# One opening product moved from POOL to DVE, the second group's sums in another order, and the last batch's end chain rewritten

## What is computed

```python
x = x + jnp.tanh(g_xattn[0]) * _L0_xattn_ref(_layernorm(x, axis=-1), ctx_4096, L0_xattn_weight)
x = x + jnp.tanh(g_ffn[0]) * _L0_ffn_ref(_layernorm(x, axis=-1), L0_ffn_router_w, L0_ffn_router_b, L0_ffn_A, L0_ffn_Bm)
```

```python
sim = jnp.stack([_cosine_sim(embedding, emb_l), _cosine_sim(embedding, embedding), _cosine_sim(embedding, emb_r)], axis=1)
...
out = jnp.einsum('bit,oi->bot', inp_unf * att, w_flat)
```

```python
topv, topi = jax.lax.top_k(probs, TOP_K)
...
h = jnp.einsum('nd,erd->ner', flat, A)
hw = h * w[:, :, None]
out = jnp.einsum('ner,eor->no', hw, Bm) * SCALING
```

## Time and profile before

| what | value |
|---|---|
| median of 3 runs | 210.16 us (210.09 to 210.34) |
| the profiled execution's own time | 210.47 us |
| its span in the profile | 208.7 us |
| PE busy, share of the span | 97% |
| DVE, POOL, ACT busy | 79%, 62%, 58% |
| moved by DMA | 26.79 MB, mean 128 GB/s |

### The profile page before, as it was taken

How to read it: one execution, slowest core, us unless ns; L and a number is a source line. 1 busy time by engine, 2 the same in 40 slices (tenths; PEclk the granted TensorE clock), 3 DMA queues, 4 the chain that set the end, 5 groups by cost and what they waited for, 6 DMA issues and landing times.

```text
span 208.7 us, 4522 instructions
## 1 busy us (share of the span) xinstructions
PE 202.4 (97%) x1466; PEld 130.9 (63%) x1466; DVE 165.6 (79%) x426; ACT 121.0 (58%) x233; POOL 129.9 (62%) x222
## 2 busy tenths in 40 slices
PE   8989999999999999999999999999999999999993
PEld 7865657566655647565655646475666666767872
DVE  3375588897979697998979698978879787878663
ACT  4677469668655673755656563845746676632331
POOL 5588654975876756476766438587557576665410
PEclk9999999999999999999999999999999999999999
DMA  6999632150443526151625323220405020202106
GB/s 192 349 375 312 237 117 85 17 190 0 147 158 121 184 102 204 64 191 50 220 81 191 106 112 100 97 108 36 168 0 195 8 104 2 100 0 114 41 0 251
DMA packets 14360, 26.79 MB, mean 128 GB/s; under 512 B 1282, under 2 KB 9602, under 8 KB 14338
## 3 DMA queue, kind: packets, MB, share of 16 engines
q1 hardware_dynamic: 14194, 26.25, 35.5%
q10 hardware_dynamic: 144, 0.26, 0.3%
HBM read 18.12 MB, written 8.39 MB: 127 GB/s over the span
## 4 chain that ended last, share of the span: by engine, by line
PE 87%; POOL 1%; issue 0%; ACT 0%; DVE 0%
PE conv_ps L1087 31%; PE hidden_ps L1138 14%; PE xT_ps L1097 7%; PE sim_ps L1066 5%; PE out_ps L1156 4%; PE hidden_ps L1008 4%; PE out_ps L1157 3%; PE out_ps L1158 3%; PE out_ps L1147 2%; PE conv_ps L1080 2%; PE conv_ps L1083 2%; PE conv_ps L1081 2%; PE xT_ps L1051 1%; PE xT_ps L1021 1%; PE conv_ps L1108 1%; PE out_ps L1183 1%
## 5 line engine op out<-in xcount | busy, mean ns | idle before, releaser
L1087 PE MATMUL conv_ps<-pt,wT 128*128 128x512 f32 x158 | 81.6, 601 | 0.0
L779 DVE TENSOR_TENSOR pt<-xn,sim_ps 128x512 f32<-128x512 f32 x96 | 60.1, 678 | 2.2 <-PE sim_ps L1066 1.6
L574 ACT ACTIVATE xT<-xT_ps 128x512 f32<-128x512 f32 x31 | 18.5, 597 | 38.9 <-PE xT_ps L1097 38.6
L1138 PEld LDWEIGHTS hidden_ps<-aT,xT 128*128 128x128 f32 x248 | 31.9, 190 | 5.5 <-issue 5.1
L1138 PE MATMUL hidden_ps<-aT,xT 128*128 128x136 f32 x248 | 33.7, 279 | 0.0
L428 POOL TENSOR_TENSOR rinv<-nmax,minus_half 128x8 f32<-128x8 f32 x16 | 26.8, 1677 | 6.4 <-DVE nmax L716 6.4
L1087 PEld LDWEIGHTS conv_ps<-pt,wT 128*128 128x128 f32 x158 | 26.1, 196 | 5.1 <-issue 3.1
L419 POOL TENSOR_TENSOR qp<-qp 128x1024 f32<-128x1024 f32 x8 | 19.0, 2381 | 14.9 <-DVE qp L701 14.9
L567 ACT ACTIVATE xn<-xt,offset,rs 128x1024 f32<-128x1024 f32 x16 | 19.8, 1237 | 7.9 <-POOL offset L439 7.6
L1097 PEld LDWEIGHTS xT_ps<-wide,x 128*128 128x128 f32 x124 | 15.3, 140 | 10.3 <-issue 7.9
L786 DVE TENSOR_TENSOR x<-conv_ps,xt 128x512 f32<-128x512 f32 x31 | 21.2, 683 | 0.6 <-PE conv_ps L1087 0.3
(11 more groups left out here) (168 smaller groups left out, 329.6 us busy)
## 6 DMA issues: line engine op xcount, KB each, us to landing
xt<-x SPq DMA_DIRECT2D x16, 512.0 KB, 3.3
et<-ctx SPq DMA_DIRECT2D x14, 514.0 KB, 4.8
out<-x SPq DMA_DIRECT2D x13, 512.0 KB, 2.7
out<-x SPq DMA_DIRECT2D x5, 256.0 KB, 2.2
aT_in<-expert_aT SPq DMA_DIRECT2D x1, 544.0 KB, 5.7
et<-ctx SPq DMA_DIRECT2D x2, 257.0 KB, 2.8
bm_in<-expert_b SPq DMA_DIRECT2D x1, 512.0 KB, 5.7
et<-ctx SPq DMA_DIRECT2D x1, 385.5 KB
```

The costliest lines, as they stand in the source:

```text
L779: nc.vector.tensor_tensor(pt[:, i, :], xn[:, n % 2, h * HALF + t:(h + 1) * HALF + t], sim_ps[:, t, :], ALU.mult).then_inc(mod_done, 1)
L1087: nc.tensor.matmul(conv_ps[h][:, :], wT[:, t * P:(t + 1) * P], pt[:, i, :], start=(t == 0), stop=(t == TAPS - 1)).then_inc(tap_done, 1)
L1138: last = nc.tensor.matmul(h_ps, xT[:, n % 2, c, :], aT[:, c, :], start=(c == 0), stop=(c == KC - 1))
```

## The change

Three parts.

1. **Product of batch 2 on DVE.** `ON_POOL` loses batch 2. DVE makes that product behind the chain that splits the first group's similarities and ahead of `rows_copy(0)`. POOL no longer waits for `split`, but for that product, then makes the product of batch 3 alone and goes on to the norms.
2. **Another order in the opening.** On PE the transpose of batch 3's sums moves ahead of `tap(1)`, `next_norms(1, 0)` ahead of `tap(4)`, and `transpose_similarities(1, 0, 4)` directly behind `tap(5)`; the eight `expert_means` matmuls are spread differently behind it. On DVE `columns_copy(3)` moves from behind `modulate(5)` to ahead of `modulate(3)`.
3. **The end.** `weigh_last` compares both indices in one instruction of 128 x 16 elements with integer ids (`ids_u`, cast once by POOL in batch 0), multiplies one comparison by its weight, and adds the other by a scalar_tensor_tensor. `finish(B - 3, 1)` leaves DVE: ACT copies that output half to `unread`, POOL adds it to `x1`, and its store waits for `late_added` and stands behind the store of the first half of batch `B - 2`. `finish(B - 2, 0)` moves ahead of `hidden_rest(B - 1)`.

```diff
-ON_POOL = (2, 3, 4, 5)
+ON_POOL = (3, 4, 5)
...
-            for n in (B - 3, B - 2):
-                for h in range(2):
-                    sp.wait_ge(out_done, 2 * n + h + 1)
-                    sp.dma_start(out[n, :, half(h)], x1[:, n % G, half(h)]).then_inc(stored[n % G], 16)
-
-            sp.wait_ge(out_done, 2 * B - 1)
+
+            for n, h in ((B - 3, 0), (B - 2, 0), (B - 3, 1), (B - 2, 1)):
+                if (n, h) == (B - 3, 1):
+                    sp.wait_ge(late_added, 1)
+                else:
+                    sp.wait_ge(out_done, 2 * n + h + (n == B - 3))
+                sp.dma_start(out[n, :, half(h)], x1[:, n % G, half(h)]).then_inc(stored[n % G], 16)
+
+            sp.wait_ge(out_done, 2 * B - 2)
             sp.wait_ge(last_out, 1)
...
                 if n == 0:
                     pool.wait_ge(ffn_in, 16 * 2)
+                    nc.gpsimd.tensor_copy(ids_u[:, :], ids[:, :]).then_inc(ids_cast, 1)
...
-            pool.wait_ge(split, 4)
-            product(2)
+            pool.wait_ge(pr_dve_done, products_up_to(2))
             product(3)
             inverse_norms(1)
...
             token_rstd(B - 1)
+
+            pool.wait_ge(hw_done, B)
+            pool.wait_ge(late_out, 1)
+            nc.gpsimd.tensor_tensor(x1[:, (B - 3) % G, half(1)], unread[:, 0, half(0)], x1[:, (B - 3) % G, half(1)],
+                                    ALU.add).then_inc(late_added, 1)
...
             expert_weights(B - 1)
+            act.wait_ge(ffn_done, 2 * (B - 3) + 2)
+            nc.scalar.activation(unread[:, 0, half(0)], ffn_ps(B - 3, 1), ACT.Copy).then_inc(late_out, 1)
             hidden_hi(B - 1)
...
-                nc.vector.tensor_copy(topf[:, i, :], topi[:, i, 0:2]).then_inc(topf_done, 1)
+                dve.wait_ge(ids_cast, 1)
+                nc.vector.tensor_tensor(chosen[:, :, :], ids_u[:, :].unsqueeze(1).to_broadcast([P, 2, E]),
+                                        topi[:, i, 0:2].unsqueeze(2).to_broadcast([P, 2, E]),
+                                        ALU.is_equal).then_inc(topf_done, 1)
                 dve.wait_ge(weights_done, 2 * B)
                 dve.wait_ge(topf_done, B)
-                for j, target in enumerate((ga, gb)):
-                    nc.vector.tensor_scalar(target[:, i, :], ids[:, :], topf[:, i, j:j + 1], weights[:, i, j:j + 1],
-                                            ALU.is_equal, ALU.mult).then_inc(picked, 1)
+                nc.vector.tensor_scalar(ga[:, i, :], chosen[:, 0, :], weights[:, i, 0:1], None, ALU.mult).then_inc(picked, 2)
                 dve.wait_ge(picked, 2 * B)
-                nc.vector.tensor_tensor(gate[:, i, :], ga[:, i, :], gb[:, i, :], ALU.add).then_inc(gate_done, 1)
+                nc.vector.scalar_tensor_tensor(out=gate[:, i, :], in0=chosen[:, 1, :], scalar=weights[:, i, 1:2],
+                                               in1=ga[:, i, :], op0=ALU.mult, op1=ALU.add).then_inc(gate_done, 1)
...
-            finish(B - 3, 1)
+            finish(B - 2, 0)
             hidden_rest(B - 1)
-            finish(B - 2, 0)
             finish(B - 2, 1)
...
             spread_similarities(0, 1)
+            transpose_context(3, 0, 0, 0)
             tap(1)
-            transpose_context(3, 0, 0, 0)
```

More of the change, by code:

```diff
@@ L135, in flamingo_kernel @@
         topf = sb("topf", [P, 2, 2])
+        ids_u = sb("ids_u", [P, E], U32)
+        chosen = sb("chosen", [P, 2, E])
         weights = sb("weights", [P, 2, 2])
@@ L281, in flamingo_kernel @@
         last_out = sem("last_out")
+        late_out = sem("late_out")
+        late_added = sem("late_added")
         last_stored = sem("last_stored")
@@ L885, in _ @@
             take(chain, 5)
+            product(2)
             rows_copy(0)
@@ L891, in _ @@
             columns_copy(2)
+            columns_copy(3)
             modulate(3)
@@ L894, in _ @@
             modulate(5)
-            columns_copy(3)
             take(partials(1), 2)
```

11 lines of the change are left out of this document (6 added, 5 removed).

## The result

| | before | after |
|---|---|---|
| median | 210.30 us (210.09 to 211.3, 12 runs) | 209.51 us (209.03 to 210.15, 12 runs) |
| the profiled execution | 210.47 us | 209.41 us |
| its span | 208.7 us | 207.7 us |

The recorded ratio of the runs is 0.9957, with a 95% interval of 0.9943 to 0.997: 0.9 us faster, between 0.6 and 1.2 (between the two medians it is 0.79). Forecast were 1.15 us and a time of 209.0 within 208.4 to 209.8.

A forecast was written before the change was run, and what follows sets the result against it. The prediction took PE to bound the middle, so a lead gained in the opening stays. Opening 0.6 plus end 0.55 makes 1.15 us, from a median of 210.16 to 209.0 us, range 208.4 to 209.8.

The forecast's parts named there:

- The four waits of the opening: PE's opening waits: batch 2's sums (unchanged), next_norms(1, 0) (0.55 us, gone), and two behind expert_means (0.2 us together, gone).
- The new wait at the transpose: Opening, PE at the transpose of batch 3's sums, no longer covered by tap(1): 0.2 us lost, bounds 0.1 and 0.4.
- The two small waits: Opening, PE behind two groups of three expert_means, ended by DVE's split and row copy: 0.1 us each, should go.
- The rival in which the wait moves to the transpose: Opening gives nothing: PE waits 0.4 us at batch 3's transpose, next_norms waits again for dr; 209.6 us, chance 0.14.
- The cost is nothing: Opening, batch 2's product on DVE: row copy 0.35 us later, PE loses nothing, 0.5 us of cover left.
- The stretch from 30 to 190 us keeps its length.: Middle, bound by PE: a lead at 30 us is still there at 190 us; a changed length proves the prediction wrong.
- The end chain, 0.16: Last batch, ga to hw one step shorter: PE gets its transpose at 202.49 instead of 202.65, gaining 0.16 us.
- The stores, 0.55 with the chain: End, last stores queue 0.66 us each; one fewer in the row, with the chain, gains 0.55 us, bounds 0.3 and 0.85.
- The rival on the other side: End, slower: a late POOL addition holds up SP's stores; 210.5 to 210.6 us at a 2.8 us addition, chance 0.05.
- Its threshold of 2.4 us: End, length of POOL's addition from which the slower case decides; the forecast took 1.25 us, upper bound 2.38.
- without the gains of both: Rival of nothing measurable: opening gives nothing and the last landing is its own cost; 210.1 us, chance 0.10.

## Why the prediction was right, point by point

Direction and time came out as forecast, the mechanism of both halves too, but that the sum fits so well is in part luck: the opening gave 0.1 more and the end 0.2 less than forecast, and two terms of the middle that the forecast didn't have nearly cancel. 1.06 us between the two profiled executions are, in the order of the program: 0.08 from an earlier start of the sums of batch 2, which differs by more than that between executions; 0.70 in the opening; 0.14 in the middle; 0.20 lost between 158 and 168, 0.18 of it by the gap; 0.35 at the end. Together 1.07.

- **The four waits of the opening.** Right for the two large ones. The transpose of batch 3's sums came at 18.22 (forecast 18.3) and its successor at 18.38 (18.46), `next_norms` at 20.96 without a wait (21.04), the similarities at 23.66 (23.73), the spreading at 25.12 (25.1). The new wait at the transpose cost the 0.2 of the forecast: the spreading frees PE 0.32 us behind its start as before, at 18.07, and `tap(1)` starts at 18.38 instead of 18.18. The two small waits gave their 0.2, but not where the forecast looked: the spreading still starts right behind DVE's row copy (25.12, the copy ends at 25.09), and the three means ahead of it take 0.90 us as before. What got shorter are the three groups of means as a whole, 2.06 us instead of 2.25, and a tap behind them, 0.07. By these, 0.55 - 0.20 + 0.09 + 0.19 + 0.07 = 0.70. DVE's product ended at 13.03 and not at 13.5, and POOL's at 15.00 and not at 15.4, where there was slack. The rival in which the wait moves to the transpose didn't happen; the run with PE's old order shows what it was up against, since there the taps wait for DVE and 0.48 us is lost.
- **"The cost is nothing" for the product on DVE.** Right in the opening, where the product is worth 0.19, and wrong behind it. The step looked for cover near the product alone. That one more product on DVE brings a gap of 0.18 us to a place at 164 us where PE waits for it is in no row of the profile before. The runs with one instruction less and six more show that it hangs on the place in the program; what makes the gap, none shows.
- **"The stretch from 30 to 190 us keeps its length."** Wrong by two small terms that nearly cancel, 0.14 gained by addresses and 0.18 lost by the gap. The text named this as a mark of failure, and it is one, of the reason and not of the size.
- **The end chain, 0.16.** It gave 0.14: the transpose of `hw` stood 3.62 us behind that matmul of the last batch (199.03) and stands 3.48 behind it. From `ga` to `hw` the 0.19 that was forecast. POOL's addition took 1.30 us (1.25).
- **The stores, 0.55 with the chain.** Mis-sized; they gave 0.35. The mechanism was right: one store less in the row takes another 0.29 off the last landing, and early stores land in 2.0 us. The 2.6 us of the Trainium skill ("DMA: Bandwidth & Descriptors", section "Anatomy of one DMA — SWDGE (gpsimd) path") come from a fit for the other kind of issue; the 2.0 us here show that it doesn't hold for this kind, not that it is wrong for its own. But the sum was of best values. The late store was issued at 203.16, 203.87 in the time of the kernel before and not 203.75; it landed in 2.05, not 2.0; and the three others follow 0.71, 0.66 and 0.69 us apart and not 0.66 each: 203.87 + 2.05 + 2.06 = 207.98, where the forecast had 207.73 and before it was 208.32. The last store landed in 2.5 us, not in the 2.2 to 2.3 that the changed profile was to show. From 204.5 to 206.5 the DMA engines of the changed kernel are full (1.01 and 1.00 at 383 and 387 GB/s), from 203.0 to 204.5 they are not (0.54 to 0.94); whether an earlier issue could use that wasn't tried.
- **The rival on the other side.** Its price was right: 1.29 us of addition costs 1.3. Its threshold of 2.4 us was near: with two additions, 2.58 us together, the end came 0.35 us later than before, counted from the sums of batch 2, so the even point is at some 2.2 us (an estimate from this one execution). What keeps the addition harmless is the wait for `hw_done`, which the prediction passed over as part of the start time; without it the whole change is worth nothing.
- **The median.** 209.51 against 209.0: 0.14 of the 0.51 is that before had a median of 210.30 over 12 runs and not 210.16 over 3; the rest is the gain, 0.79 between the medians against 1.15. (Of the rivals' times one was added up wrongly: without the gains of both, only the 0.16 of the chain is left, 210.0 and not 210.1. Nothing hangs on it.)

So the opening, with nothing to spare on three engines, held to 0.1 us, and the end, counted on a queue model with round numbers, lost 0.2.

## What to carry to other kernels

Where an edit makes an engine free earlier, write down every start up to the next shared point from the rows and see whether each engine arrives: here this gave five starts of PE to 0.1 us. Queues of stores want the opposite care, since each landing has its own spread and they add up. And in a program without slack, a difference of 0.1 to 0.2 us far from the edit can come from the place of instructions or from addresses: test it by an edit that changes nothing else before giving it a reason.

## What the runs showed of the hardware that was not expected

- A gap of about 0.18 us on DVE that stands at a place in its program and not at an instruction (a step of 0.79 us from 163.31 to 164.10, against 0.61 without it).
- 7 to 8 ns less for a matmul of 128 x 512 (398 to 391 and 390) when buffers lie 96 bytes further on.
- A DVE operation of 0.29 us that took 1.35 us beside a POOL addition. Before, the same had stood in small: POOL's `gate` at 38.64 took 1.00 us instead of 0.20 beside DVE's product from 38.34 to 39.58.
- The granted clock fell in one execution and not in another of the same opening: 0.68 and 0.50 in the two windows from 11 to 15 us in the run with one store less, 1.00 in both in the changed kernel, whose program differs from it only at the end. PE had idled 0.27 us ahead of the sums of batch 1 in the first and 0.41 us at 10.69 in the second, so that idle time alone doesn't tell the two apart.
